# A hardware loop over ten of sixteen batches, and router logits with the operands swapped

## The reference, cut to what matters

```python
x = x + tanh(g_xattn) * attention(layernorm(x), ctx)     # 16 heads of 32, causal, softmax
# the feed-forward part on t = layernorm(x), 4096 tokens
scores = softmax(t @ router_w)                            # 8 experts
topk_w, topk_idx = top_k(scores, 6)
f_all  = (silu(t @ w_gate[e]) * (t @ w_up[e])) @ w_down[e]   # every expert e, 512 -> 256 -> 512
y = sum of the 6 picked f_all, weighted by topk_w
y = y + (silu(t @ ws_gate) * (t @ ws_up)) @ ws_down          # shared, 512 -> 512 -> 512
x = x + tanh(g_ffn) * y
```

## Time and profile before

| | |
|---|---|
| median of three executions | 2075.33 us |
| the profiled execution, its own time | 2075.33 us |
| its span, first to last instruction | 2073.6 us |
| granted TensorE clock, mean | 0.983 |
| attention stage | about 0 to 660 us |
| experts | about 660 us to the end |
| blocks 0 to 3 made ready | 663 to 744 us |
| blocks 4 to 7 made ready | 1336 to 1429 us |

### The profile page before, as it was taken

One profiled execution on the slowest core, in us unless ns is written; L12 is line 12 of the kernel. 1 busy time (PEld: TensorE's weight loads), 2 busy tenths in 40 slices (PEclk: granted clock), 3 DMA queues, 4 the chain that ended last, 5 costly groups with the idle time before them and its releaser, 6 DMA issues.

```text
span 2073.6 us, 33203 instructions
## 1 busy us (share of the span) xinstructions
PE 2032.7 (98%) x12288; PEld 1717.6 (83%) x12288; DVE 1150.8 (55%) x2773; ACT 789.6 (38%) x1966; POOL 190.4 (9%) x395
## 2 busy tenths in 40 slices
PE   6999999999997999999999999999999999999999
PEld 6899999999886888888888888788888888888887
DVE  5888888898887644333433343465333343433333
ACT  4777777777774521111211111243111111121111
POOL 3221321222211100000000000010000000000000
PEclk9999999999997899999999999989999999999999
DMA  7555655646543110000100010231001000101002
GB/s 208 134 132 140 144 137 139 148 123 151 136 118 129 50 31 21 21 26 25 30 20 20 20 30 21 61 102 41 21 21 31 21 21 20 30 20 27 14 1 81
DMA packets 117509, 138.38 MB, mean 67 GB/s; under 512 B 9728, under 2 KB 91648, under 8 KB 117376
## 3 DMA queue, kind: packets, MB, share of 16 engines
q1 hardware_dynamic: 117376, 136.63, 24.9%
HBM read 69.49 MB, written 16.78 MB: 42 GB/s over the span
## 4 chain that ended last, share of the span: by engine, by line
PE 65%; DVE 1%; DMA 1%; issue 0%; POOL 0%; ACT 0%; SPq 0%; POOLq 0%; ACTq 0%
PE gate_up L1168 42%; PE down L1187 21%; PE gate_up L1151 1%; PE down L1137 1%; DMA acc<-x_between 0%; DMA out<-acc 0%; ACT xn L917 0%; DVE norm_stats L888 0%; POOL norm_newton L97 0%; DVE xt_lo L1039 0%; DVE acc L1094 0%; SPq L978 0%; DVE h L1080 0%; POOL norm_newton L95 0%; ACT h_hi L1011 0%
## 5 line engine op out<-in xcount | busy, mean ns | idle before, releaser
L1168 PE MATMUL gate_up<-xt_hi,e_hi 128*128 128x512 f32 x1280 | 508.2, 397 | 0.0
L1168 PE MATMUL gate_up<-xt_hi,e_lo 128*128 128x512 f32 x1280 | 507.4, 396 | 0.0
L1168 PE MATMUL gate_up<-xt_lo,e_hi 128*128 128x512 f32 x1280 | 507.1, 396 | 0.0
L1080 DVE TENSOR_TENSOR h<-gate_up,silu 128x512 f32<-128x512 f32 x160 | 110.6, 691 | 560.8 <-PE gate_up L1168 551.4
L1008 ACT ACTIVATE silu<-gate_up 128x512 f32<-128x512 f32 x160 | 95.8, 599 | 575.8 <-PE gate_up L1168 575.6
L1094 DVE SCALAR_TENSOR_TENSOR acc<-down,scale,acc 128x512 f32<-128x512 f32 x320 | 238.9, 749 | 119.4 <-PE down L1187 113.2
L1168 PEld LDWEIGHTS gate_up<-xt_lo,e_hi 128*128 128x128 f32 x1280 | 241.3, 189 | 58.6
L1168 PEld LDWEIGHTS gate_up<-xt_hi,e_hi 128*128 128x128 f32 x1280 | 241.5, 189 | 58.2
L1168 PEld LDWEIGHTS gate_up<-xt_hi,e_lo 128*128 128x128 f32 x1280 | 241.3, 189 | 57.8
L1011 ACT CAST h_hi<-h 128x512 fp32r<-128x512 f32 x160 | 99.3, 620 | 462.3 <-DVE h L1080 462.3
L1187 PE MATMUL down<-e_hi,h_hi 128*128 128x512 f32 x640 | 256.1, 400 | 0.9 <-DVE acc L1094 0.9
(11 more groups left out here) (126 smaller groups left out, 3370.3 us busy)
## 6 DMA issues: line engine op xcount, KB each, us to landing
k_stack<-k_hi SPq DMA_DIRECT2D x128, 128.0 KB, 2.6
q_stack<-q_hi SPq DMA_DIRECT2D x128, 128.0 KB, 2.6
w_raw<-in_w_gate SPq DMA_DIRECT2D x20, 512.0 KB, 3.8
w_raw<-in_w_up SPq DMA_DIRECT2D x20, 512.0 KB, 3.8
w_raw<-in_w_down SPq DMA_DIRECT2D x20, 512.0 KB, 3.6
c_in<-in_ctx_t SPq DMA_DIRECT2D x16, 512.0 KB, 3.7
x_in<-in_x SPq DMA_DIRECT2D x16, 512.0 KB, 3.9
k_stack<-k_lo SPq DMA_DIRECT2D x64, 128.0 KB, 2.6
```

The lines of the kernel that those rows point to most:

```text
L1080: dve.tensor_tensor(h[f][:], gu_ps[f][:, 1, :], silu[f][:], ALU.mult).then_inc(h_made, 1)
L1168: ins = pe.matmul(gu_ps[f][:, which, :], (hi, lo)[a][:, c, f * P:(f + 1) * P], (xt_hi, xt_lo)[b][:, blk, c, :], start=(i == 0), stop=(i == ...
```

## The change

It has two parts. In the attention stage, iterations -1 to 2 and 13 to 16 stay unrolled, and iterations 3 to 12 run as five turns of a hardware loop with two iterations in its body, on every engine. In the experts, the router columns become the weights and the 512 tokens of a block the moving data, so that the logits come out with the 16 columns as partitions (8 products, into the gate bank `gu_ps[0][:, 0]`); ScalarE copies them to SBUF (`copy_logits`); and TensorE turns them back in four products with a matrix `fold` that also adds the two halves (`transpose_back`), into the up bank. `transpose_back` stands after the second of the four tiles of `down`, or right behind the logits where the step has no `down`. The maximum and the subtraction read the result in PSUM, and up of step n+2 waits for `shift_made`.

```diff
+    FIRST, PAIRS = 3, 5
+
     def iterations(eng, run):
-        for i in range(-1, B + 1):
+        for i in range(-1, FIRST):
+            run(At(0, 2, i))
+        with eng.Fori(0, PAIRS) as r:
+            for u in range(2):
+                run(At(r, 2, FIRST + u))
+        for i in range(FIRST + 2 * PAIRS, B + 1):
             run(At(0, 2, i))
...
+    fold = sb("fold", [2 * E, E])
-    logits = sb("logits", [P, BT, E])
+    logits_t = sb("logits_t", [2 * E, BLK])
...
-    logits_ps = gu_ps[0][:, 1, 0:BT * 2 * E].rearrange("p (t x e) -> p t x e", t=BT, x=2)
+    logits_ps = gu_ps[0][0:2 * E, 0, :]
+    back_ps = gu_ps[0][:, 1, 0:BT * E].rearrange("p (t e) -> p t e", t=BT)
...
+        dve.tensor_tensor(fold[:], ident[0:2 * E, 0:E], ident[0:2 * E, E:2 * E], ALU.add).then_inc(r_lo_made, 1)
...
+                def copy_logits(k):
+                    act.wait_ge(logits_done, k + 1)
+                    wait(act, logits_back, k)
+                    act.copy(logits_t[:], logits_ps).then_inc(logits_made, 1)
...
                     if stands(n + 1):
                         hidden(n + 1, 1)
+                    if k is not None:
+                        copy_logits(k)
...
-                    dve.wait_ge(logits_done, k + 1)
-                    dve.tensor_reduce(logits[:], logits_ps.rearrange("p t x e -> p t e x"), AX.X, ALU.add).then_inc(logits_made, 1)
-                    dve.wait_ge(logits_made, k + 1)
-                    dve.tensor_reduce(top[:], logits[:], AX.X, ALU.max).then_inc(route_chain, 1)
+                    dve.wait_ge(logits_back, k + 1)
+                    dve.tensor_reduce(top[:], back_ps, AX.X, ALU.max).then_inc(route_chain, 1)
                     dve.wait_ge(route_chain, ROUTE_STEPS * k + 1)
-                    dve.tensor_tensor(shift[:], logits[:], top[:].unsqueeze(2).to_broadcast([P, BT, E]),
+                    dve.tensor_tensor(shift[:], back_ps, top[:].unsqueeze(2).to_broadcast([P, BT, E]),
                                       ALU.subtract).then_inc(shift_made, 1)
...
                     if k == 0:
-                        pe.wait_ge(r_lo_made, 1)
+                        pe.wait_ge(r_lo_made, 2)
+                    for c in range(C):
+                        for i, part in enumerate((xt_lo, xt_hi)):
+                            ins = pe.matmul(logits_ps, r_parts[:, c].rearrange("p x e -> p (x e)"), part[:, k % NB, c, :],
+                                            start=(c == 0 and i == 0), stop=(c == C - 1 and i == 1))
+                    ins.then_inc(logits_done, 1)
+
+                def transpose_back(k):
+                    pe.wait_ge(logits_made, k + 1)
                     for t in range(BT):
-                        for c in range(C):
-                            for i, part in enumerate((xt_lo, xt_hi)):
-                                ins = pe.matmul(logits_ps[:, t], part[:, k % NB, c, t * P:(t + 1) * P], r_parts[:, c],
-                                                start=(c == 0 and i == 0), stop=(c == C - 1 and i == 1))
-                    ins.then_inc(logits_done, 1)
+                        ins = pe.matmul(back_ps[:, t, :], logits_t[:, t * P:(t + 1) * P], fold[:], start=True, stop=True)
+                    ins.then_inc(logits_back, 1)
...
-                            pe.wait_ge(logits_made, logits_before + 1)
+                            pe.wait_ge(shift_made, logits_before + 1)
...
                         ins.then_inc(down_done, 1)
+                        if k is not None and t == 1:
+                            transpose_back(k)
...
                     if stands(n):
                         down(n, k)
+                    elif k is not None:
+                        transpose_back(k)
```

More of the change, by code:

```diff
@@ L812, in experts @@
     gate_done, up_done, down_done = sem("gate_done"), sem("up_done"), sem("down_done")
-    e_xt_done, logits_done = sem("e_xt_done"), sem("logits_done")
+    e_xt_done, logits_done, logits_back = sem("e_xt_done"), sem("logits_done"), sem("logits_back")
     x1_v = x1.rearrange("(k t p) d -> k p t d", p=P, t=BT)
```

## The result

The change makes the kernel slower: 2098.31 us median (2096.86 to 2099.81, four runs) beside 2073.93 us of the kernel before on the same chip (2070.87 to 2075.34, four runs), a ratio of 1.0125 with a 95% interval of 1.011 to 1.0139. The forecast was 2069.8. The span went from 2073.6 to 2098.4 us, 24.8 us more. To place them I read where TensorE starts the last `scores` product of attention: at 639.59 us before and 674.58 us after. So attention takes **35.0 us more**, and the experts give back 10.2.

What follows compares the result with a forecast made beforehand. TensorE, busy 98% of the span, was taken as the bound, with VectorE a close second in attention. 2075.3 - 18.5 (experts) + 13 (attention loop) = 2069.8 us; own range 2062 to 2078, outer range 2055 to 2100.

Steps and rivals of the forecast that it cites:

- The jump back: Attention loop: 1 us for each of five turns, bounded by 0 and 2.6 us, the nearest row of a transfer.
- rival 2: Attention loop: all engines find their code gone at each jump, 6 us a turn, kernel 2094.8 us; chance 0.10.
- register waits: Attention loop, VectorE: 0.05 us for each of some 16 waits, 0.8 us per iteration, 8 us in ten.
- Rival 1: Attention loop: register work slows every VectorE wait by 0.11 us, VectorE becomes the bound, kernel 2106.8 us; chance 0.17.
- The place at head 12: Attention, once per iteration: a VectorE delay passes undiminished to TensorE, whose product waits for `pt_lo` behind the normalising operations.
- The turned products: Experts, TensorE: four small float32 products per block turn the logits back and fold the halves, 1.0 us per block.
- The clock: Experts: with dense products in place of thin ones TensorE's clock stays up behind the logits, giving back 14.0 us.
- Rival 4: Experts: the clock falls all the same, so they give only 6.4 us and the kernel takes 2081.9 us; chance 0.07.
- The first group of blocks: Experts, first four blocks of 512 tokens getting router logits: 10.3 us less, from shorter logits and clock, less the fold.
- The second group: Experts, last four blocks, where the path leaves TensorE for store, load, statistics and normalisation: 8.2 us less.
- They move by 3.8 us too: Experts: the eighth block's statistics and normalisation come 3.8 us earlier; TensorE gains 6.0 us there in place of 7.9.
- 3 (a free loop): Attention: the loop costs nothing, TensorE's margins covering it, and the kernel takes 2056.8 us; chance 0.18.

Runs made afterwards that it cites:

- the placed loop: Attention loop alone with 50 instructions of satisfied waits ahead of it on TensorE, against the kernel before: 2093.68 us beside 2073.53.
- the 50 instructions: Satisfied waits ahead of TensorE's loop; with TensorE alone looping and these, every other engine unrolled as before: 2079.84 us beside 2075.52.
- the run with 16 thin products: The kernel before with half its logits products per block, the low part of the rows left out: 2056.27 us, a single execution.
- the stores first: New logits alone, new buffers placed last, SyncE's stores and x1 loads ahead of its weight loads, against the kernel before: 2057.89 us beside 2074.66.
- the padded whole change: The whole change with 50 instructions of satisfied waits ahead of the loop on TensorE and 32 on VectorE: 2072.63 us beside 2074.07 before.

## Why the prediction was wrong, step by step

**The step that failed** is "The jump back is bounded by 0 and by the nearest row of a transfer, 2.6 us; I take 1 us for each of five turns". It measured 8.7 us for each of four, 35.0 in all where the term was 5 and its bound 13. The bound took a jump for one transfer with nothing behind it. In fact TensorE waits twice in a row, 2.4 to 2.7 and 3.2 to 4.0 us, and about 4 us of work at half clock follow after it stood nearly idle for 6 us; VectorE's wait, worth about 3 us by itself, lies partly beside these. The cause is the one of rival 2, code that must come again, but on TensorE and VectorE alone and not on all engines. It had 0.10. That its 2094.8 us come near 2098.3 is in part luck: its 30 us for the jumps stand beside 35, its 8 us for register waits beside almost nothing, and its savings of 18.5 beside 10.2. It is luck too that 35 us for attention and 2098.3 us lie just inside the outer bounds of the prediction (0 to 35, 2055 to 2100): they were kept that wide for register waits.

The Trainium skill (Runtime: NRT & Kernel Launch, Instruction fetch mechanics) says that a taken branch whose target is outside the fetched window forces a fetch before execution goes on. The trace agrees: TensorE's gaps at the four jumps come with code packets that the placed loop doesn't have (91 against 55). I cited the rule and gave it little, because the experts' loops run without a gap, but these bodies are shorter on TensorE (1184 instructions against 1639) and on VectorE (177 against 340). The page gives TensorE room for 2048 instructions in blocks of 256; an estimate from it has the body of 1639 fit everywhere, while the runs show that it depends on the place. If a block is 256 instructions, 1639 touch seven or eight blocks, by place, and 340 on VectorE, in packets half as large, three or four; that seven are held and eight aren't, and three and not four, fits all the runs but was not measured by itself. Nor was TensorE alone in the loop without the 50 instructions, so the split of the 8.7 us between the two engines is a difference of runs with all engines.

**Register waits**, the term of 8 us, cost next to nothing: with VectorE alone in the loop the iterations away from a jump take 38.16 to 38.20 us, and before 38.13 (the 38.3 of the prediction is one of the few longer ones). VectorE's rows in the loop and in the kernel before have the same distances; in the kernel before

```profile
305.28 0.28 DVE L550 CUSTOM_DVE_ANT_0 probs<-scores,mask 128x128 f32<-128x128 f32 x1
...
309.66 0.18 DVE L521 RECIPROCAL row_inv<-row_sum 128x8 f32<-128x8 f32 x1
...
311.33 0.69 DVE L510 TENSOR_TENSOR t_lo<-bank,t_hi 128x512 fp32r<-128x512 f32 x1
```

and with VectorE alone in the loop, away from a jump

```profile
349.76 0.28 DVE L561 CUSTOM_DVE_ANT_0 probs<-scores,mask 128x128 f32<-128x128 f32 x1
...
354.14 0.19 DVE L532 RECIPROCAL row_inv<-row_sum 128x8 f32<-128x8 f32 x1
...
355.81 0.69 DVE L521 TENSOR_TENSOR t_lo<-bank,t_hi 128x512 fp32r<-128x512 f32 x1
```

4.38 and 6.05 us from the first row in both. The 0.11 us by which the `acc` pairs differ belong to something else in them, which no run separates (their operand with an address in a register is one candidate). Rival 1 is refuted by this. The place at head 12 of which I made so much did not move.

**The logits on TensorE** were right: 1.84 to 2.04 us for the predicted 1.87, and 3.59 for 3.7 in the first block.

**The turned products** were right at 1.0 us, 0.245 each. With the four passes of the Trainium skill (FP8 and Floating Point Precision, TensorE Precision Notes, on true FP32) the estimate was 1.75 us per block. The trace has eight records for the four products, which fits more than one pass each, but the time is that of the term taken.

**The clock** was right: 1.00 behind the logits, and 24 products in 5.6 to 5.8 us. Rival 4 is refuted, and the run with 16 thin products points to the length of the thin stretch, the first block apart.

**The first group of blocks** was predicted at 10.3 us less (9.1 saved + 7.2 of clock - 6.0 for the fold) and gave 9.9. Here and for the second group one execution stands beside one: in the 13 kernels with the expert part of before, the stretch from the last scores to `down` of step 2 takes 114.1 to 116.2 us, and that from `down` of step 36 to `down` of step 41 takes 111.3 to 116.5.

**The second group** was predicted at 8.2 less and gave 5.6. Part of the 2.6 us between them is within that spread. The step that looks too large is "They move by 3.8 us too". In the chain before, the store and the load ahead of the seventh block were

```profile
1364.41 4.86 DMA out<-acc
...
1369.29 5.74 DMA acc<-x_between
```

and after, the links ahead of the seventh and of the eighth block are

```profile
1387.55 6.25 DMA out<-acc
1393.82 5.45 DMA acc<-x_between
...
1412.39 4.99 DMA out<-acc
1417.40 5.85 DMA acc<-x_between
```

The path now leaves TensorE for such links at more places, and they don't get shorter with TensorE's work: TensorE stands 1.17 and 0.99 us ahead of the transposes of these two blocks. With the stores first neither wait is there, the chain has no such link, and the group takes 104.5 us beside 107.6 without. That is 10.8 less than the 115.3 of before, about TensorE's own account of 10.1 in the prediction (6.3 saved + 6.8 of clock - 3.0 for the fold). So, as far as one execution of each can show it, the order of SyncE's transfers is what kept this group short of that account.

**Unforeseen**: 5.3 us in the steady steps, from `down` at 5.60 us in place of 5.51 in 54 of 72. The run with the new buffers behind the others has 5.51 again in every second step and is 2.9 us faster. The other 2 us or so are there because the second half of before has 5.51 in every step, which other kernels with the same addresses have in one half or in none. Why an address changes a product's rate, and what else does, stays open.

The sum by the measured terms: -9.9 - 5.6 + 5.3 + 35.0 = +24.8 us, the difference of the spans. Of the rivals, 3 (a free loop) holds for ScalarE, GpSimd and SyncE, and for the other two in a good place, as far as its jumps go: the padded whole change misses its 2056.8 by the pads (attention takes 6.6 us more than before), the longer `down` and the store chain.

## What to carry to other kernels

A hardware loop is priced by whether its body's code stays in each engine's instruction memory, and that must be asked engine by engine: count the compiled body's instructions, compare the code queues' packets with those of the unrolled kernel, and look for gaps marked "issue" just behind the jump. If the body is near the limit, some satisfied waits ahead of the loop can decide between 9 us and next to nothing per jump, and a loop on only those engines that need it costs nothing on the others. And when an operation is swapped in, look also at what its new buffers push to other addresses, and split a change of two parts into its parts before judging either.

## What the runs showed of the hardware that I had not expected

- A jump back can cost TensorE two separate waits of 2.4 to 2.7 and 3.2 to 4.0 us, and the clock falls to 0.50 behind them for some 4 us.
- The same loop costs 8.7 us per jump or next to nothing depending on 50 instructions ahead of it, with 91 or 55 code packets.
- VectorE's code comes in packets of 8 KB and TensorE's of 16 KB; a body of 340 instructions on VectorE is already long enough to be fetched again (65 packets against 45).
- Waits on registers cost VectorE less than 0.1 us in an iteration of 38.13, but satisfied waits in a row cost TensorE 0.11 us per instruction.
- 24 products take 5.51 or 5.60 us at a clock of 1.00 in both. With two small buffers declared ahead of others they take 5.60 in every steady step; with the old addresses a half of the experts alternates between the two or has 5.51 throughout, and what decides that isn't known.
